# Graph attention on Trainium2: in the heads layer, the sum of rows and edges in four parts, the second maxima in two, one weighting product moved

## The reference

```python
h_edge = ((atom[src] + bond) @ W).reshape(-1, H, D)
h_node = (atom @ W).reshape(-1, H, D)
el = jnp.einsum('ehd,hd->eh', h_edge, attn_l)
er = jnp.einsum('nhd,hd->nh', h_node, attn_r)
s = el + er[dst]
s = jnp.where(s > 0, s, NEG_SLOPE * s)
smax = jax.ops.segment_max(s, dst, num_segments=N)
ex = jnp.exp(s - smax[dst])
denom = jax.ops.segment_sum(ex, dst, num_segments=N)
alpha = ex / denom[dst]
ft = jax.ops.segment_sum(h_edge * alpha[..., None], dst, num_segments=N)
```

## Time and profile before

| what | value |
|---|---|
| median of three runs | 8733.55 us (8731.82 to 8734.4) |
| the profiled execution | 8733.21 us |
| its span | 8731.5 us |
| busy: PE, DVE, ACT, POOL | 4763.8, 6710.5, 4432.3, 6328.2 us |
| heads layer, about | 90 to 2260 us of the span |
| the heads gathers, POOL | 1664, 1590.7 us busy |

### The profile page before, as it was taken

The page is one execution under the profiler, slowest core; times in us unless marked ns, Lnnn a source line. Parts: engine busy times, 40 slices in busy tenths (PEclk is TensorE's granted clock), DMA queues, the critical chain, the costliest instruction groups (busy, mean ns, idle before and its releaser), DMA issues. The chain is left out here.

```text
span 8731.5 us, 120061 instructions
## 1 busy us (share of the span) xinstructions
PE 4763.8 (55%) x23534; PEld 4288.2 (49%) x23534; DVE 6710.5 (77%) x12205; ACT 4432.3 (51%) x11726; POOL 6328.2 (72%) x6675
## 2 busy tenths in 40 slices
PE   5777777777555555555545555555554444444444
PEld 5666666666444444444444444444443444444444
DVE  6888888888577777777767777777776777777777
ACT  5777777777444444444434444444443444444443
POOL 4777777777077777777767777777776777777776
PEclk8666666666655555555555555555555555555555
DMA  2222222222121222222212222222211222222221
GB/s 76 57 58 57 57 58 56 58 58 56 63 32 32 32 32 32 32 32 32 32 28 32 32 32 32 32 32 32 32 32 30 35 35 35 35 35 35 35 35 31
DMA packets 576283, 348.39 MB, mean 40 GB/s; under 512 B 451757, under 2 KB 452653, under 8 KB 576239
## 3 DMA queue, kind: packets, MB, share of 16 engines
q0 software_dynamic: 212992, 229.61, 16.3%
q1 hardware_dynamic: 362527, 118.16, 5.8%
q10 hardware_dynamic: 720, 0.17, 0.0%
HBM read 319.62 MB, written 27.76 MB: 40 GB/s over the span
## 5 line engine op out<-in xcount | busy, mean ns | idle before, releaser
L1610 POOL DMA_INDIRECT plain_rows_in<-table,plain_idx x4992 | 4723.7, 946 | 1523.8 <-issue 1523.2
L1858 PE MATMUL plain_ps_sums<-plain_rows_in,plain_prob 128*128 x10080 | 2298.8, 413 | 0.3 <-ACT plain_prob L1816 0.3
L1858 PEld LDWEIGHTS plain_ps_sums<-plain_rows_in,plain_prob 128*128 128x128 f32 x10080 | 2234.0, 330 | 27.8 <-ACT plain_prob L1816 0.9
L1029 POOL DMA_INDIRECT heads_rows_in<-h_in,heads_idx x1664 | 1590.7, 956 | 588.2 <-issue 507.4
L1816 ACT ACTIVATE plain_prob<-plain_prob 128x2048 f32<-128x2048 f32 x312 | 595.8, 1910 | 1969.7 <-DVE plain_prob L1742 1969.7
L1880 PE MATMUL plain_ps_max<-ident,plain_column_max 128*128 128x128 f32 x312 | 148.0, 474 | 1803.9 <-DVE plain_column_max L1722 1803.9
L1807 ACT ACTIVATE plain_ps_score<-plain_mask,plain_rows_in 128x128 f32<-128x128 f32 x3744 | 1110.9, 350 | 0.0
L1880 PEld LDWEIGHTS plain_ps_max<-ident,plain_column_max 128*128 128x128 f32 x312 | 56.9, 182 | 1895.7 <-DVE plain_column_max L1722 1895.7
L1742 DVE TENSOR_TENSOR plain_prob<-plain_prob,plain_ps_max 128x2048 f32<-128x2048 f32 x312 | 714.0, 2288 | 267.5 <-PE plain_ps_max L1885 267.5
L1664 DVE SCALAR_TENSOR_TENSOR plain_mask<-plain_mask,plain_ps_er 128x2048 f32<-128x2048 f32 x315 | 720.6, 2287 | 193.0 <-PE plain_ps_er L1833 192.8
L1807 ACT ACTIVATE plain_score_sb<-plain_mask,plain_rows_in 128x128 f32<-128x128 f32 x1248 | 398.5, 390 | 902.6 <-DMA plain_rows_in<-table,plain_idx 902.6
(11 more groups left out here) (250 smaller groups left out, 8659.5 us busy)
## 6 DMA issues: line engine op xcount, KB each, us to landing
plain_rows_in<-table,plain_idx POOLq DMA_INDIRECT x4992
heads_edges<-in_edge_attr SPq DMA_DIRECT2D x108, 512.0 KB
heads_rows_in<-h_in,heads_idx POOLq DMA_INDIRECT x1664
plain_own<-table SPq DMA_DIRECT2D x324, 33.5 KB, 2.3
table<-plain_out_sb SPq DMA_DIRECT2D x208, 33.5 KB
plain_idx<-in_src SPq DMA_DIRECT2D x324, 8.0 KB
plain_dst_ids<-in_dst SPq DMA_DIRECT2D x324, 8.0 KB
plain_unit_par<-unit_floats SPq DMA_DIRECT2D x324, 1.0 KB
```

The costliest lines, as they stand in the source:

```text
L1029: gp.indirect_dma_start(rows_in[h][:, t, :], None, table[:, :], bass.IndirectOffsetOnAxis(ap=idx[h][:, t:t + 1], axis=0)).then_inc(gathere ...
L1610: gp.indirect_dma_start(rows_in[h][:, t, :], None, table[:, :], bass.IndirectOffsetOnAxis(ap=idx[h][:, t:t + 1], axis=0)).then_inc(gathere ...
L1858: ins = te.matmul(sums[h % 2], prob[h % 2][:, t, :], rows, start=t == 0, stop=t == Q - 1)
```

## The change

Four edits, all in what DVE does in the heads layer:

1. The sum of rows and edges leaves `take_rows` and is made in four parts of 4 columns (128x256) each. The first stands behind the local destinations, the second behind the shift matrix and the freshness, the third behind the one-hot, the fourth between `head_max` of head 0 and `finish`. The signal to POOL that the rows are taken comes with the fourth.
2. `localize` is cut into two: the local destinations first, and shift matrix and freshness (`place`) behind the first part of the sum.
3. The maximum of the two parts in SBUF in `head_max` is made in two parts of 128x256, each of which is waited for.
4. `weigh_rows` is cut into two: the product of head 0 comes ahead of `node_maxima`, the product of head 1 and the copy of the weights stay behind it.

```diff
@@ -1040,7 +1040,7 @@
             @block.vector
             def _(ve):
                 rounds = unit_rounds(ve)
-                STEPS = 24
+                STEPS = 26
 
                 for h in range(RING):
                     ve.sem_inc(rows_taken[h], 1)
@@ -1059,11 +1059,14 @@
                 def localize(k, h):
 
                     ve.wait_ge(meta_loaded[h], 32 * k + 32)
+                    ve.tensor_scalar(dst_local[:, :], dst_ids[h][:, :], unit_par[h][:, 0:1], None,
+                                     ALU.subtract).then_inc(local_made, 1)
+
+                def place(h):
+
                     by = unit_par[h][0:NB, 1:2]
                     ve.tensor_scalar(shift_mat[h][:, :], con.lag[:, :], by, None, ALU.is_equal)
                     ve.tensor_scalar(fresh[:, :], con.node_id[:, :], by, float(NB), ALU.add, ALU.is_ge)
-                    ve.tensor_scalar(dst_local[:, :], dst_ids[h][:, :], unit_par[h][:, 0:1], None,
-                                     ALU.subtract).then_inc(local_made, 1)
 
                 def build_onehot(n, h):
 
@@ -1078,8 +1081,13 @@
                     ve.tensor_tensor(scores_sum[:, :, :], edge_scores[:, :, :], rows_in[h][:, :, D:D + heads],
                                      ALU.add).then_inc(scores_ready, 1)
                     ve.wait_ge(edges_loaded[h], 16 * i + 16)
-                    ve.tensor_tensor(edges[h][:, :, :], edges[h][:, :, :], rows_in[h][:, :, 0:D], ALU.add
-                                     ).then_inc(rows_taken[h], 1)
+
+                def add_rows(h, g):
+
+                    cols = slice(g * GROUP, (g + 1) * GROUP)
+                    ins = ve.tensor_tensor(edges[h][:, cols, :], edges[h][:, cols, :], rows_in[h][:, cols, 0:D], ALU.add)
+                    if g == CHUNKS - 1:
+                        ins.then_inc(rows_taken[h], 1)
 
                 def begin(i, h, step):
 
@@ -1090,11 +1098,12 @@
                 def head_max(n, hd, step):
 
                     ve.wait_ge(masked_made, 2 * heads * n + 2 * hd + 1)
-                    low, middle_part, high = (slice(k * HALVED, (k + 1) * HALVED) for k in range(3))
-                    step(ve.tensor_tensor(top[:, 0:HALVED, :], masked[:, hd, low, :], ps_masked[hd], ALU.max))
+                    step(ve.tensor_tensor(top[:, 0:HALVED, :], masked[:, hd, 0:HALVED, :], ps_masked[hd], ALU.max))
                     ve.wait_ge(masked_made, 2 * heads * n + 2 * hd + 2)
-                    step(ve.tensor_tensor(top[:, HALVED:, :], masked[:, hd, middle_part, :], masked[:, hd, high, :],
-                                          ALU.max))
+                    for k in range(2):
+                        low, high = (slice(HALVED * m + k * HALVED // 2, HALVED * m + (k + 1) * HALVED // 2)
+                                     for m in (1, 2))
+                        step(ve.tensor_tensor(top[:, low, :], masked[:, hd, low, :], masked[:, hd, high, :], ALU.max))
                     step(ve.tensor_reduce(column_max[:, hd, :], top[:, :, :].rearrange("p t n -> p n t"), AX.X,
                                           ALU.max))
                     ve.sem_inc(columns_maxed, 1)
@@ -1133,14 +1142,21 @@
                     step(ve.scalar_tensor_tensor(max_before[:, :], fresh[:, :].to_broadcast([NB, heads]), -BIG,
                                                  carried_max, ALU.mult, ALU.add))
 
-                def weigh_rows(n, h):
-
-                    rows = edges[h]
+                def weigh(h, hd):
+
+                    ve.tensor_tensor(weighted[:, :, hd * part:hd * part + D], edges[h][:, :, 0:D],
+                                     bcast(weights[:, :, hd], 2, D), ALU.mult)
+
+                def weigh_first(n, h):
+
                     ve.wait_ge(weights_made, n + 1)
                     ve.wait_ge(aggregated, n + 2)
-                    for hd in range(heads):
-                        ve.tensor_tensor(weighted[:, :, hd * part:hd * part + D], rows[:, :, 0:D],
-                                         bcast(weights[:, :, hd], 2, D), ALU.mult)
+                    weigh(h, 0)
+
+                def weigh_rest(h):
+
+                    for hd in range(1, heads):
+                        weigh(h, hd)
                     ve.tensor_copy(weighted[:, :, D::part], weights).then_inc(rows_weighted, 1)
 
                 def edge_logits(n, step):
@@ -1156,6 +1172,7 @@
                     ve.tensor_scalar(logits[:, :, :], logits[:, :, :], 0.0, None, ALU.min).then_inc(logits_made, 1)
 
                 localize(0, 0)
+                place(0)
                 build_onehot(0, 0)
                 ve.wait_ge(w_loaded, 5 * 16)
                 step = own_steps(ve, w_made)
@@ -1171,21 +1188,28 @@
                         take_rows(i, h, n)
                         begin(i, h, step)
                         localize(i + (h == RING - 1), after(h))
+                        add_rows(h, 0)
+                        place(after(h))
+                        add_rows(h, 1)
                         ve.wait_ge(weights_made, n + 1)
                         ve.wait_ge(aggregated, n + 1)
                         build_onehot(n + 1, after(h))
+                        add_rows(h, 2)
                         head_max(n, 0, step)
+                        add_rows(h, 3)
                         finish(n, step)
                         head_max(n, 1, step)
+                        weigh_first(n, before(h))
                         node_maxima(n, h, step)
-                        weigh_rows(n, before(h))
+                        weigh_rest(before(h))
                         edge_logits(n, step)
                         carry_maxima(step)
                         assert step.taken() == STEPS, step.taken()
                 n = ve.snap(RING * rounds)
                 step = own_steps(ve, chain, ve.snap(n * STEPS))
                 finish(n, step)
-                weigh_rows(n, RING - 1)
+                weigh_first(n, RING - 1)
+                weigh_rest(RING - 1)
                 finish(ve.snap(n + 1), step)
 
             @block.scalar
```

## The result

The changed kernel took 8786.07 us (median of four runs, 8785.33 to 8788.39) against 8732.95 us before: a ratio of 1.0061, 95% interval 1.0047 to 1.0076. It is 53 us slower; 8702 us were forecast, in a range of 8686 to 8715.

The account below looks back on a forecast made before the run. The heads layer was taken as bound by the chain through DVE and ACT, with POOL right behind. The chain shortens, POOL binds, and its 30.85 us lead is gained: 8733.2 - 31 = 8702 us, range 8686 to 8715.

Parts of the forecast that it names:

- The last carries the end of the loop: Heads layer, last of a round's four units: its loop end was part of the 81.94 us round, with no added cost.
- Chain: DVE and ACT path of a heads-layer unit: 0.19 + 0.50 - 1.13 = -0.44 us, round from 81.94 to 80.2 us.
- Room ahead of ACT: DVE's 0.60 us wait for ACT at the second maximum would hide +0.5 us (up to +0.9) of added work.
- POOL becomes the bound at about 80.7 us a round: Heads layer: with the chain at 80.2 us, POOL's gathers set the round at 80.74 us; last take 30.85 us earlier.
- POOL's losses would stay about as they were: Gathers held off by DVE's two-input operations: 0.82 us a round kept, between bounds of none and 1.3 us.
- Slower rival: Pieces and gathers meet at the port in the heads layer: +68 us, 8801 us; chance 0.08.
- The rule of the Trainium skill against pieces under 512 elements: Fixed latency per DVE operation: the sum's four pieces would cost +0.47 us instead of +0.23, using up the room.
- units last over 20.3 us with the lead still growing: Heads-layer sign that the forecast is wrong, the chain not shortened; POOL's lead at the last take was 30.85 us.

Follow-up runs that it names:

- shifts of 0 and 128: The changed kernel as it is, and with 128 one-element DVE memsets ahead of the heads layer's loop: 8786.07 and 8784.92 us.
- 64 and 192: The changed kernel with 64 or 192 one-element DVE memsets ahead of the heads layer's loop: 8702.1 and 8703.14 us, one execution each.
- the sum alone: Kernel before with only the sum in four parts and the shift matrix later, plus 64 memsets ahead of the loop: 8733.49 us against 8731.3.
- the product alone: Kernel before with only head 0's weighting product ahead of the node maxima, plus 64 memsets ahead of the loop: 8756.17 us against 8731.3.
- without the halves: Changed kernel with 64 memsets ahead of the loop, but the second maximum whole (128x512) as before: 8711.26 us against 8731.3 for the kernel before.
- all parts: The whole changed kernel with 64 memsets ahead of the loop, timed in rounds: 8699.17 us against 8732.15 for the kernel before, ratio 0.9962.

## Why the prediction was wrong

**The step that failed** is a term that the sum put at nothing: "Where do the 81.94 us go? ... The last carries the end of the loop". I took the 0.67 us at the loop's end as a constant and priced the 32 instructions that the change adds to a round at their own duration only, never asking what the branch costs when the loop's code no longer lies in what the engine holds. It cost 106.7 us in 25 stops for 16.7 before: 90 us against a forecast gain of 31. The Trainium skill has the rule ("Runtime: NRT & Kernel Launch", Instruction fetch mechanics): a taken branch whose target isn't in the current window forces a fetch of it. The trace agrees (126 packets more, 3.6 us more at each branch). The page's window of two blocks of 256 instructions does not fit, for by it shifts of 0 and 128 could not both stop while 64 and 192 run; here the measurement decides. I had looked into the durations of operations and not at what the longer loop does to its own code.

Point by point:

- *Chain:* -0.44 us a unit forecast, a round of 80.2 us. From the second maximum to the node maxima it went as worked out (0.92 and 1.34 us), the node maxima's wait is gone, and without the 3.6 us of the stop the measured round is 83.9 - 3.6 = 80.3 us. This part was right.
- *Room ahead of ACT:* hidden, as forecast (8733.49 us with the sum alone), but its term was too large: +0.5 us of the 0.60 were to be used and 0.1 to 0.3 left, and 0.39 us were left at head 1, behind a new wait at head 0. The sum in parts took none of the room.
- *POOL becomes the bound at about 80.7 us a round:* right once the stop is away (80.6), and the time with it, 8699 us, is 3 us under the forecast 8702. That POOL's losses would stay about as they were was a guess between two ends, and it was luck that it hit (1588.3 us busy for 1590.7): in the other versions above they went up by 9 to 52 us.
- *In the changed kernel itself* POOL never became the bound. It ran ahead as before, until it waited for the indices of a unit to come (134.7 us of such waits for 80.8).
- *Slower rival:* it had the sign, at a chance of 0.08, but not the mechanism: it had POOL's collisions, and in the changed kernel gathers were even a little shorter. The collisions do decide between the versions, though: 8756 with the product alone, 8711 without the halves, 8699 with all parts.
- *The rule of the Trainium skill against pieces under 512 elements* ("VectorE: DVE Perf Modes", on the TRN2 errata) did not decide: the trace agrees with its sizes (0.42 us for 256 elements), and the halves give back more at the gathers than their 0.19 us cost (8711 us without them).
- *What would show it:* the sign "units last over 20.3 us with the lead still growing" did appear: 20.98 us in the mean, and a lead of 2274.6 - 2238.1 - 2.6 = 33.9 us for 30.85. But what it was to mean, that the chain was not shortened, was wrong: the excess sits in the last unit of each round, 23.4 to 24.4 us for 20.6 before, while the other three are 0.2 to 0.5 us shorter than before. Listing the waits without releaser would have named the loop's end at once.

The sum with what was missing: 25.75 rounds x (80.2 + 3.6 - 81.94) = 48 us more, 8781 us, where 8786 were measured.

## What to carry to other kernels

Count the instructions that a change adds to an engine's loop, and look at the rows of the instruction queue and at the idle time behind the backward branch before and after; here some 30 instructions more, even ones ahead of the loop, cost more than the change gives, and 64 more ahead of the loop gave it back. When an engine that ran ahead becomes the bound, the beat of all others is tied to it: test parts of a change together too, since the product that shortens the chain made this kernel slower without the sum in parts.

## What the runs showed of the hardware

- DVE's loop of 330 recorded instructions runs without a stop or with one, by its place alone, with a period of 128 instructions (shifts 0 and 128 against 64 and 192). The idle time at the loop's end is then 3.9 to 4.8 us a pass in the mean (97.9 to 120.7 us in 25 passes), of which 0.67 us is there without the stop too. All twelve kernels fit a rule by which three pages of 8192 bytes have to hold the loop; that rule and the start in the page (64 to 86) are inferred, and no run gave the exact start. That the extra packets are DVE's is inferred too, from their number going with the stops. The Trainium skill ("Runtime: NRT & Kernel Launch", Instruction fetch mechanics) has blocks of 256 instructions; the packets of 8192 bytes and the period of 128 differ from it, and here they decide.
- The port: a gather that starts while an operation with two SBUF inputs runs waits for its end less about 0.13 us. It held from 0.09 us up to 1.01 us (1186.61 above: 1186.52 + 1.23 - 1186.61 - 0.13 = 1.01).
